# Two layer norms joined to the layer streams behind them, and another order of splits in all four norms

## What is computed

```python
def _layernorm(x, axis=-1, eps=1e-05):
    m = jnp.mean(x, axis=axis, keepdims=True)
    v = jnp.var(x, axis=axis, keepdims=True)
    return (x - m) / jnp.sqrt(v + eps)

x = x + attn_a(_layernorm(x))        # softmax(y y^T) y
x = x + ffn(_layernorm(x), ...)      # 2 layers: shift, qkv, l2norm, rotary, local attention, wo, LN, gated GELU
x = x + attn_b(_layernorm(x), ...)   # weighted values
x = x + ffn(_layernorm(x), ...)
```

## Time and profile before

| | us |
|---|---|
| median of 3 runs | 1656.61 (1654.36 to 1656.76) |
| the profiled execution | 1658.8 |
| its span in the trace | 1657.0 |
| mean granted TensorE clock, share of full speed | 0.958 |

### The profile page before, as it was taken

The page is one execution under the profiler, slowest core; times in us unless marked ns, Lnnn a source line. Parts: engine busy times, 40 slices in busy tenths (PEclk is TensorE's granted clock), DMA queues, the critical chain, the costliest instruction groups (busy, mean ns, idle before and its releaser), DMA issues.

```text
span 1657.0 us, 46687 instructions
## 1 busy us (share of the span) xinstructions
PE 1451.6 (88%) x19015; PEld 1145.1 (69%) x19015; DVE 1271.5 (77%) x1688; ACT 1289.0 (78%) x1952; POOL 1170.1 (71%) x778
## 2 busy tenths in 40 slices
PE   5998986889999999999987666889999999999986
PEld 3777864777777777777774453667777777777764
DVE  6776666778888888888864865878888888888863
ACT  4876865688888888888875855788888888888874
POOL 3010015778999999999962645889989899999960
PEclk8999997899999999999997877999999999999998
DMA  4100003665666557565640002666565656566542
GB/s 110 35 8 2 0 13 59 122 116 113 116 126 114 115 120 124 118 109 118 116 87 7 1 7 65 130 119 120 119 117 119 111 120 121 115 116 120 115 76 57
DMA packets 350305, 149.09 MB, mean 90 GB/s; under 512 B 298306, under 2 KB 326028, under 8 KB 350092
## 3 DMA queue, kind: packets, MB, share of 16 engines
q1 hardware_dynamic: 350092, 146.11, 45.3%
HBM read 23.10 MB, written 2.10 MB: 15 GB/s over the span
## 4 chain that ended last, share of the span: by engine, by line
PE 33%; POOL 20%; ACT 18%; DVE 12%; issue 8%; DMA 5%; SPq 2%; DVEq 0%; POOLq 0%; ACTq 0%
POOL t L1203 9%; POOL t L1209 6%; PE PS L195 6%; PE PS L197 5%; PE PS L196 5%; DMA t<-t 5%; DVE t L1054 4%; POOL HL L1227 3%; ACT t L946 3%; ACT L996 2%; ACT L946 2%; PE PS L678 2%; PE PS L390 2%; PE PS L392 2%; PE PS L391 2%
## 5 line engine op out<-in xcount | busy, mean ns | idle before, releaser
L1203 POOL TENSOR_TENSOR t<-t 128x1024 f32<-128x1024 f32 x128 | 439.2, 3431 | 102.5 <-DVE t L1054 100.7
L1209 POOL TENSOR_TENSOR t<-t 128x512 f32<-128x512 f32 x256 | 320.6, 1274 | 18.7 <-POOL t L1203 0.4
L1048 DVE TENSOR_REDUCE t<-t 128x16 f32<-128x1024 f32 x128 | 156.1, 1220 | 113.0 <-ACT t L860 113.0
L195 PE MATMUL PS<-wqh,HH 128*128 128x512 f32 x384 | 173.6, 452 | 50.5 <-DVE t L1054 25.7
L860 ACT ACTIVATE t<-PS 128x1024 f32<-128x1024 f32 x128 | 131.4, 1027 | 91.3 <-PE PS L197 90.9
L1054 DVE SCALAR_TENSOR_TENSOR t<-t,PS 128x1024 f32<-128x1024 f32 x128 | 155.2, 1213 | 21.4 <-ACT t L867 21.4
L1083 DVE TENSOR_REDUCE t<-PS 128x8 bf16<-128x1024 f32 x128 | 156.1, 1219 | 18.4 <-PE PS L652 18.4
L703 PE MATMUL PS<-t 128*64 128x65 f32 x4096 | 147.5, 224 | 23.5 <-DVE t L1114 21.7
L1064 DVE TENSOR_TENSOR t<-t 128x1024 f32<-128x1024 f32 x128 | 164.0, 1281 | 4.4
L873 ACT CAST t<-t 128x1024 bf16<-128x1024 f32 x128 | 133.2, 1041 | 36.6 <-POOL t L1209 34.4
L1071 DVE TENSOR_TENSOR t<-t,PS 128x1024 bf16<-128x1024 f32 x128 | 155.3, 1214 | 5.2 <-ACT PS L880 5.1
(11 more groups left out here) (250 smaller groups left out, 3690.1 us busy)
## 6 DMA issues: line engine op xcount, KB each, us to landing
t<-t SPq DMA_DIRECT2D x254, 130.0 KB, 2.3
t<-in_c_rope SPq DMA_DIRECT2D x128, 128.0 KB, 2.9
t<-yT SPq DMA_DIRECT2D x112, 128.0 KB
t<-t SPq DMA_TRANSPOSE x304, 3.3
t<-in_L_attn_a_x SPq DMA_DIRECT2D x4, 512.0 KB, 6.9
out_x<-t SPq DMA_DIRECT2D x8, 256.0 KB, 3.4
t<-yT SPq DMA_DIRECT2D x16, 127.8 KB
t<-in_L_ffn_wqkv SPq DMA_DIRECT2D x2, 768.0 KB, 4.4
```

The source lines that it names most:

```text
L195: e.matmul(o, ah, bh, start=not more, stop=False, skip_group_check=True)
L1048: e.e.tensor_reduce(ss[:, 0:16], BL.sq, AX.X, ALU.add).then_inc(S.la_ss, 1)
L1203: e.e.tensor_tensor(BL.tc.rearrange("p (x h) d -> p x h d", x=2), BL.qn.rearrange("p (x h) d -> p x h d", x=2), sin.to_broadcast([128, 2, ...
L1209: e.e.tensor_tensor(tv[:, :, 32 * s:32 * s + 32], tv[:, :, 32 * s:32 * s + 32], BL.tc[:, :, 32 * (1 - s):32 * (1 - s) + 32], ALU.add).then ...
```

## The change

Two things are changed.

1. **The norms k = 1 and k = 3 lose their own stage.** Their instructions move into `layers_pe`, `layers_act`, `layers_dve` and `layers_pool`, in pieces `norm(part)` set between those of the stream's first two steps. They use four banks for centred chunks (2 to 5) and two for variances (6, 7) where there were five and three (`BESIDE`), since `project` needs banks 0 and 1, and lie in buffers of the stream that its first tiles don't need yet (`BM`). A barrier stands now only ahead of the joined stage. Tile 0's `project` no longer waits for all eight chunks of the norm, only for its own chunk. `first_weights` moves from step 0 to step 1.
2. **In all four norms** DVE splits chunks 1 and 3, puts chunk 0, splits 5, puts 1, splits 7, then puts the rest. POOL's low part of chunk 4 waits for DVE's of chunk 3, and that of chunk 6 for DVE's of chunk 5. The five weight instructions of norm k = 2 come after the put of chunk 3.

```diff
+        APART = Names(cens=5, cen=lambda c: c % 5, vars=3, var=lambda c: 5 + c % 3)
+        BESIDE = Names(cens=4, cen=lambda c: 2 + c % 4, vars=2, var=lambda c: 6 + c % 2)
...
         def plain_pool(e, src, k):
             for c in range(0, NCH, 2):
                 e.wait_ge(S.pl_hi, 4 * k + c // 2 + 1)
+                if c >= 4:
+                    e.wait_ge(S.pl_lo_dve, 4 * k + c // 2)
                 e.e.tensor_tensor(chunk(HL, c), chunk(src, c), chunk(HH, c).bitcast(F32),
                                   ALU.subtract).then_inc(S.pl_lo_pool, 1)
...
-        def normed_dve(e, stage, k, j, src, twice, more=lambda e: None):
-
-            others_ended(e, stage)
-            plain_dve(e, src, j)
+        def normed_dve(e, stage, k, j, src, more=lambda e: None):
+            others_ended(e, stage)
+            plain_dve(e, src, j, (1, 3))
+            layernorm_dve(e, k, BN, range(1), twice=True)
+            plain_dve(e, src, j, (5,))
+            layernorm_dve(e, k, BN, range(1, 2), twice=True)
+            plain_dve(e, src, j, (7,))
+            layernorm_dve(e, k, BN, range(2, 4), twice=True)
             more(e)
+            layernorm_dve(e, k, BN, range(4, NCH), twice=True)
+            dve_end(e)
...
         def layers_sp(e, stage, u, k):
-            others_ended(e, stage - 1)
+            others_ended(e, stage)
...
                 if C >= NCH:
                     e.wait_ge(S.ff_out, NC * u + C - NCH + 1)
+                else:
+                    e.wait_ge(S.ln_put, NCH * k + C + 1)
                 shifted(BL.ysl, C, S.ys_l)
...
-        def layers_pe(e, stage, u):
-            others_ended(e, stage)
+        def layers_pe(e, stage, u, k):
+            others_ended(e, stage)
+            norm(range(7))
...
                 if on(0):
                     project(s)
+                if s == 0:
+                    norm(range(7, NCH + 2))
                 if on(2):
                     values(s - 2)
                 feed_bank_7(s)
-                if u == 0 and s == 0:
+                if u == 0 and s == 1:
                     first_weights()
...
+            plain_act(e, x1, k)
+            norm(range(5))
             high_for_attention(0)
-            others_ended(e, stage)
+            norm(range(5, 7))
             for s in range(STEPS):
...
                 if on(0):
                     squares(s)
+                if s == 0:
+                    norm(range(7, 8))
...
                 if on(0):
                     rnorms(s)
+                if s == 0:
+                    norm(range(8, NCH + 2))
...
+            plain_dve(e, x1, k, (1, 3))
+            norm(range(1))
+            plain_dve(e, x1, k, (5,))
+            norm(range(1, 2))
+            plain_dve(e, x1, k, (7,))
+            norm(range(2, 5))
...
                 if on(1):
                     normed(s - 1)
                     rope(s - 1)
+                if s == 1:
+                    norm(range(6, NCH))
...
                 if on(0):
                     norms(s)
+                if s == 0:
+                    norm(range(5, 6))
```

More of the change, by code:

```diff
@@ L251, in plain_act, with plain_dve @@
                 e.e.copy(chunk(HH, c), chunk(src, c)).then_inc(S.pl_hi, 1)
-        def plain_dve(e, src, k):
-            for c in range(1, NCH, 2):
+        def plain_dve(e, src, k, part):
+            for c in part:
                 e.e.tensor_copy(chunk(HH, c), chunk(src, c)).then_inc(S.pl_hi_dve, 1)
@@ L262, in plain_pool, with layernorm_pe @@
                 e.wait_ge(S.pl_hi, 4 * k + c // 2 + 1)
+                if c >= 4:
+                    e.wait_ge(S.pl_lo_dve, 4 * k + c // 2)
                 e.e.tensor_tensor(chunk(HL, c), chunk(src, c), chunk(HH, c).bitcast(F32),
                                   ALU.subtract).then_inc(S.pl_lo_pool, 1)
-        def layernorm_pe(e, k, B, ready, first_bank0=lambda c: None):
-            for c in range(NCH + 2):
+        def layernorm_pe(e, k, B, ready, part=range(NCH + 2), banks=APART):
+            for c in part:
                 if c < NCH:
@@ L270, in layernorm_pe @@
                     ready(c)
[L271 to L275, removed]
+                    if c >= banks.cens:
+                        e.wait_ge(S.ln_put, n - banks.cens + 1)
+                    e.e.matmul(PS[:, banks.cen(c), :], cenr[:, :], chunk(HH, c), start=True, stop=False)
+                    e.e.matmul(PS[:, banks.cen(c), :], cenr[:, :], chunk(HL, c), start=False,
                                stop=True).then_inc(S.ln_cen, 1)
@@ L279, in layernorm_pe, with layernorm_act @@
                     e.wait_ge(S.ln_sq, n + 1)
-                    if c - 2 >= 3:
-                        e.wait_ge(S.ln_ln, n - 3 + 1)
-                    e.e.matmul(PS[:, var_bank(c - 2), :], avg, B.sq[(c - 2) % 3], start=True,
+                    if c - 2 >= banks.vars:
+                        e.wait_ge(S.ln_ln, n - banks.vars + 1)
+                    e.e.matmul(PS[:, banks.var(c - 2), :], avg, B.sq[(c - 2) % 3], start=True,
                                stop=True).then_inc(S.ln_var, 1)
-        def layernorm_act(e, k, B):
-            for c in range(NCH + 2):
+        def layernorm_act(e, k, B, part=range(NCH + 2), banks=APART):
+            for c in part:
                 if c < NCH:
@@ L291, in layernorm_act @@
                         e.wait_ge(S.ln_var, n - 3 + 1)
[L292 removed]
+                    e.e.activation(B.sq[c % 3], PS[:, banks.cen(c), :], ACT.Square).then_inc(S.ln_sq, 1)
                 if 2 <= c < NCH + 2:
@@ L336, in normed_pool @@
             plain_pool(e, src, j)
[L337 to L341, removed]
+            for c in range(NCH):
+                e.wait_ge(S.ln_hi, NCH * twice + c + 1)
+                e.e.tensor_tensor(chunk(HL, c), chunk(yT, c), chunk(HH, c).bitcast(F32),
+                                  ALU.subtract).then_inc(S.ln_lo, 1)
             pool_end(e)
@@ L598, in layers_sp, with norm @@
                     past(s - 2)
-        def layers_pe(e, stage, u):
+        def layers_pe(e, stage, u, k):
             others_ended(e, stage)
+            def norm(part):
+                layernorm_pe(e, k, BM, lambda c: split_ready(e, c, k), part, BESIDE)
+            norm(range(7))
             hi = lambda i: TS * u + i
@@ L846, in layers_pe, with layers_act, norm @@
             pe_end(e)
-        def layers_act(e, stage, u):
+        def layers_act(e, stage, u, k):
+            others_ended(e, stage)
             hi = lambda i: TS * u + i
+            def norm(part):
+                layernorm_act(e, k, BM, part, BESIDE)
             def first_weights():
@@ L1025, in layers_act, with layers_dve, norm @@
             act_end(e)
-        def layers_dve(e, stage, u):
+        def layers_dve(e, stage, u, k):
             others_ended(e, stage)
+            def norm(part):
+                layernorm_dve(e, k, BM, part, BESIDE)
             hi = lambda i: TS * u + i
```

96 lines of the change are left out of this document (45 added, 51 removed).

## The result

The changed kernel takes 1646.78 us (median of 4 runs, 1645.49 to 1648.64) where the one before took 1656.68 beside it; the ratio is 0.9945 with a 95% interval of 0.9929 to 0.9961, that is 9.1 us less. The profiled execution took 1647.32 us.

What follows compares the result with a forecast made beforehand. POOL and the chain behind it were taken to pace the streams. From the 1656.6 median, -13.6 us for both streams and +5.9 for norms k = 0 and k = 2 gave -7.7, so 1648.9 us; range 1641.0 to 1655.0.

Steps and rivals of the forecast that it cites:

- the likeliest one: The forecast itself: streams 13.6 us less, norms k = 0 and k = 2 5.9 more, 1648.9 us; chance 0.55.
- Tile 0's chain: Start of each joined stream: early put 0 lets `project(0)` start 6.7 us earlier, some 15 us after ACT's first cast.
- The leads: Both streams, POOL's start on tile 1: 6.8 us earlier each, the middle of 6.1 and 7.5.
- the upper bound of 7.5: Lead at POOL's start on tile 1 with both projections at 2.4 GHz and POOL as the bound: 7.5 us.
- I cost the move at nothing: Moving `first_weights` (1.77 us on DVE) from step 0 to step 1 of a stream: no cost.
- The lead lasts: Both streams: the lead tile 1 has on POOL reaches the end, no outside clock holding tiles back; 6.8 us each.
- Rival C: First stream steps wait for transposing DMAs on SP; streams gain 6 us together, norms take it back: 1656.6; chance 0.06.
- Norm k = 0: New split order moves put 2 from 26.95 to about 30.2, and the norm takes +3.0 us.
- Norm k = 2: DVE waits ahead of put 0, split 7 alternates with POOL; put 2 2.8 us late, norm +2.9 us.
- Rival A: Norms k = 0 and k = 2: new order costs nothing, POOL having too little to do; 1643.0; chance 0.17.
- B: Streams: half-clock stretch lost in u = 0 (1643.3, chance 0.08) or one more in u = 1 (1654.5, chance 0.10).
- D: Steps 3 to 9 of each stream: the clock falls once more, +3.5 us, 1660.1; chance 0.04.

Runs made afterwards that it cites:

- the new order alone: The kernel before with the new order of splits in all four norms, nothing joined: 1660.66 us, ratio 1.0038.
- POOL kept off: The changed kernel with POOL's low parts of the results in norms k = 0 and k = 2 waiting for DVE's split 7: 1642.57 us, ratio 0.9919.
- 1641.29 us: The changed kernel with the old order of splits in norms k = 0 and k = 2, the joining kept: 1641.29 us, ratio 0.991.
- the delay of 6.4 us: The kernel before with twelve settings of 512 columns on DVE behind self-attention's last addition: 1662.87 us, ratio 1.0041.

## Why the prediction held, and where it was off

The forecast was 1648.9 us, 7.7 less than before; measured were 1646.8 and 9.1 less (6.5 to 11.8). The time was in the range, the sign was right, and the case was the likeliest one. Point by point:

- **Tile 0's chain: right.** `project(0)` was due some 15 us after ACT's first cast and came at 14.87. The steps on the way hit within some tenths: project by 6.85 us earlier for a forecast of 6.7. Put 2 did hold centring 6, as worked out; with the old order, where it doesn't come as late, `project(0)` waits for the shifted chunk instead and starts at 15.2, so the two ways to it are about equally long.
- **The leads: too small.** Forecast 6.8 us for each stream, from bounds of 6.1 and 7.5. On tile 1 they are 8.0 and 6.9, on tile 2 8.1 and 8.4, on tile 10 7.6 and 8.1. That 6.9 is near the forecast is luck of the place where one looks: tile 0's projection at 2.4 GHz gave 7.4 us on tile 0, and the 1.0 us by which POOL's table is held stands ahead of tile 1 and is given back within it. The mis-sized term is the upper bound of 7.5. It counted the idle time that POOL had ahead of tile 1 (0.46 us); POOL also had 0.83 us ahead of tile 2, of which 0.1 to 0.5 are left in the joined executions of stream u = 1. And in u = 0 POOL isn't the bound on tile 1: it waits 2.7 us there for the chain, and `normed` of tile 1 comes 29.7 us after ACT's first cast where it came at 37.7, 8.0 us earlier.
- **`first_weights`, "I cost the move at nothing": not settled.** Before, it stood ahead of tile 0's `normed`: POOL came to tile 0 at 32.1 us in u = 0 and 28.9 in u = 1, 3.2 us later. On tile 1 that was 39.1 - 36.1 = 2.9. Now both start tile 0 at 21.5, and on tile 1 u = 0 is 31.0 - 29.2 = 1.8 later. That looks like 1.1 us gained; but on tile 2 the difference is 2.9 us before and 3.2 now, nothing gained. No run moved `first_weights` alone.
- **The lead lasts: right.** 15.3 us on tile 63 for 14.9 on tile 1. Rival C is excluded.
- **Norm k = 0: right in kind, 0.45 us too much in this execution.** Put 2 was to be 3.2 us late and was 2.8 (29.82 - 15.07 against 26.95 - 14.96), the stage +2.55 for +3.0. The mean of the three executions with the new order less that of the six with the old one is +3.0.
- **Norm k = 2: the sum close, the working wrong.** "So the delay stays: +2.9" failed. Put 2 was late by 2.05 us, not 2.8: Exp 0 came half a us earlier, and the rest of split 7's meeting was a little shorter. But before, the five weight instructions stood ahead of put 2, and now they stand behind it: from 912.96 to 915.57 they add 2.61 us, of which 0.84 is one instruction of two columns held by POOL (1.01 us for 0.17). From put 2 to the end of the last cast the rest takes 8.73 us where it took 9.89, since POOL ran out of work meanwhile. 2.05 + 2.61 - 1.16 = 3.50, the measured 3.51. I compared two instructions of the same name on two sides of moved work.
- **Rival A: excluded** by the new order alone (+6.3 us) and by the splits' 1.50 and 1.64 us.
- **Rivals B and D: the mechanism exists, but not as I set it up.** I took the low stretch of stream u = 0 for a property of the kernel before. It depends at least in part on the execution: of the five not joined one has it in full, three have half of it and one has none; of the five joined one has half of it (POOL kept off: 0.66 in 300 to 305) and four have none, but each of the five has a short one some 46 us behind ACT's first cast (3.4 us at half clock; in the changed kernel's two executions 0.84 and 0.82, 0.95 and 0.71 in 280 to 285 and 285 to 290). So the sign that I had named for B and D did appear, a stretch that goes and one that comes in steps 3 to 9, and the median still came out nearer to the forecast than to B's 1643.3. My price for it was too high as well: I put 5.6 us on the stretch, all of POOL's idle time there, but between an execution with all of it and one with none tile 8 moves by 4.1 us and the stage by 3.6. The profiled execution I started from had it, so some 3.6 us of the difference between the two profiles in stream u = 0 are no gain by the change. My sum did not count on them.
- **Not foreseen: weighted values +0.9 us.** The ten executions show two values, 54.8 (four) and 55.7 to 56.0 (six), and they go with the clock: where the stage takes 54.8 us, the granted clock is at half for 20.0 to 20.7 us of it, where it takes 55.7 for 22.5 to 23.4, and in the one of 56.0 for 26.6. Whether the change has a part in it is open. All four with the short time have the old order of splits in norm k = 2, and all four with the new order have the long one, but so have two with the old order (1641.29 us, and the delay of 6.4 us).

The means give -15.3 for the streams on tile 63, +3.0 and +3.7 for the norms: -8.6, within the interval of the measured 9.1. The forecast had -13.6 and +5.9: both terms were too small, by 1.7 and 0.8 us, and the two errors in part cancel.

## What to carry to other kernels

Where a barrier makes the first tile of a pipeline wait for a whole stage of which it needs one chunk, running the stage into the pipeline gives the wait back (here 7 to 8 us for each of two streams), and a pipeline that one engine paces keeps nearly all of it to the end. Don't put ready work of an engine behind a wait so that something else may come first, where another engine can hold that work up: the wait stays empty (3.7 us here), and the work then meets the other engine (2.0 us). When work moves past an instruction, compare that instruction's time only together with the work that has changed sides. A lead read on one tile can be off by what has only moved across the start of that tile (here 1.0 us); read it on the next tiles too. Profile a kernel twice before a stretch at a low clock is taken for its own.

## What the runs showed of the hardware

- An instruction of two columns on DVE (0.17 us alone) took 1.01 us beside POOL's subtraction; not only wide casts are held. POOL is held too: a product of 256 columns took 1.72 us beside DVE's `rope` instead of 0.72, and one of 1024 columns 2.38 us without `rope` beside it instead of 3.42.
- Executions of the same stream code that agree to 0.1 us on tile 1 (39.0 to 39.1 in five executions) lie 4.4 us apart on tile 10 (114.7 to 119.1), with the granted clock at 1.00 in 305 to 310 in one and 0.55 in the other. The kernel before alone spans 1649.11 to 1660.35 us in 19 runs.
- Around PE's pause of 4.21 us the changed kernel's clock was 1.00 throughout the pause and 0.50 only behind it, while PE worked. In the kernel before it fell within the pause of 4.75 us ahead of `project(0)` (1.00 in 1004 to 1005, 0.61 in 1005 to 1006; PE starts at 1006.49). So a pause of about the same length was seen with either.
